# A selective scan on one core: state sums in 64x64 tiles, skip term on TensorE, gating from PSUM on VectorE

## The reference, cut to what matters

```python
xz = einsum('bld,ed->ble', x, inW); xi, z = split(xz, 2)
u = silu(causal_conv4(xi) + convB)
dt, Bm, Cm = split(u @ xpW.T, [8, 24])
delta = softplus(dt @ dtW.T + dtB);  A = -exp(Alog)
h[t] = h[t-1] * exp(delta[t] * A) + delta[t] * u[t] * B[t]      # per channel and state
y[t] = sum over the 16 states of h[t] * C[t]
y = (y + u * Dp) * silu(z);  out = y @ outW.T
```

## Time and profile before

| | us |
|---|---|
| median of three runs (3236.65 to 3239.31) | 3238.32 |
| the profiled execution | 3238.96 |
| its span, first to last instruction | 3237.2 |
| busy in the span: PE, PEld, DVE, ACT, POOL | 2481.1, 1545.4, 2175.4, 1557.8, 1433.7 |
| TensorE clock granted, mean over the span | 0.887 |
| first scan of the Mamba stage starts, last one starts | 1646.3, 2692.5 |

### The profile page before, as it was taken

How to read it: one execution, slowest core, us unless ns; L and a number is a source line. 1 busy time by engine, 2 the same in 40 slices (tenths; PEclk the granted TensorE clock), 3 DMA queues, 4 the chain that set the end, 5 groups by cost and what they waited for, 6 DMA issues and landing times. The chain is left out here.

```text
span 3237.2 us, 54004 instructions
## 1 busy us (share of the span) xinstructions
PE 2481.1 (77%) x18923; PEld 1545.4 (48%) x18923; DVE 2175.4 (67%) x3838; ACT 1557.8 (48%) x2529; POOL 1433.7 (44%) x1159
## 2 busy tenths in 40 slices
PE   4888657764777589899689999999999996553603
PEld 3555435553555455555345555555555553332303
DVE  4787547885777545555356767767677774887688
ACT  4888425553777522222265556555555542221360
POOL 5555235554222100000058877778777874332001
PEclk9999777885999889999899999999999998765756
DMA  1000010000000100000122222122221211000000
GB/s 38 1 0 1 8 34 17 15 10 4 1 0 0 45 1 0 0 0 0 31 66 70 69 67 63 60 74 65 67 63 62 71 61 35 20 13 8 0 0 26
DMA packets 108701, 94.26 MB, mean 29 GB/s; under 512 B 11136, under 2 KB 104976, under 8 KB 108432
## 3 DMA queue, kind: packets, MB, share of 16 engines
q1 hardware_dynamic: 108560, 92.26, 9.4%
HBM read 83.32 MB, written 2.62 MB: 27 GB/s over the span
## 5 line engine op out<-in xcount | busy, mean ns | idle before, releaser
L1919 POOL TENSOR_TENSOR mam_h<-mam_h,mam_c_all 128x1024 f32<-128x1024 f32 x256 | 632.4, 2478 | 187.4 <-DVE mam_h L1987 187.4
L1987 DVE TENSOR_TENSOR_SCAN mam_h<-mam_decay,mam_ps_b 128x1024 f32<-128x1024 f32 x256 | 578.2, 2279 | 199.7 <-PE mam_ps_b L1633 195.5
L1640 PE MATMUL mam_ps_y<-mam_h,all_ident 128*128 128x512 f32 x1024 | 501.4, 613 | 6.1 <-DVE mam_y L1963 6.1
L1803 ACT ACTIVATE mam_decay<-mam_delta,mam_a_neg 128x508 f32<-128x508 f32 x512 | 331.3, 709 | 65.6 <-DVE mam_h L1987 65.5
L1633 PEld LDWEIGHTS mam_ps_b<-mam_diag,mam_duT 64*128 64x128 f32 x4096 | 250.1, 188 | 214.2 <-issue 151.6
L1633 PE MATMUL mam_ps_b<-mam_diag,mam_duT 64*128 64x128 f32 x4096 | 299.0, 286 | 20.5 <-DVE mam_h L1987 16.6
L1640 PEld LDWEIGHTS mam_ps_y<-mam_h,all_ident 128*128 128x128 f32 x1024 | 179.0, 190 | 200.5 <-issue 164.4
L519 DVE TENSOR_REDUCE at_top<-at_ps_s 128x4 f32<-128x512 f32 x256 | 175.0, 683 | 120.1 <-PE at_ps_s L359 120.1
L1234 ACT ACTIVATE moe_silu<-moe_ps_g 128x512 f32<-128x512 f32 x144 | 86.0, 597 | 291.9 <-PE moe_ps_g L1181 263.3
L437 ACT COPY at_probT<-at_ps_t 128x512 f32<-128x512 f32 x256 | 145.1, 588 | 119.0 <-PE at_ps_t L344 118.6
L1184 PE MATMUL moe_ps_u<-moe_ynT,moe_w_up 128*128 128x512 f32 x288 | 159.6, 637 | 36.7 <-DVE moe_hidden L1317 36.7
(11 more groups left out here) (346 smaller groups left out, 4925.3 us busy)
## 6 DMA issues: line engine op xcount, KB each, us to landing
mam_c_all<-mam_c_rows SPq DMA_DIRECT2D x256, 256.0 KB, 3.4
all_x_all<-in_x SPq DMA_DIRECT2D x8, 256.0 KB, 4.8
ret_xg<-all_x_all SPq DMA_DIRECT2D x32, 64.0 KB, 1.8
ret_ctx<-in_ctx SPq DMA_DIRECT2D x32, 64.0 KB, 1.9
mam_xg<-all_x_all SPq DMA_DIRECT2D x8, 256.0 KB, 4.0
xat_xg<-all_x_all SPq DMA_DIRECT2D x8, 256.0 KB, 2.4
xat_ctx<-in_ctx SPq DMA_DIRECT2D x8, 256.0 KB, 2.9
out<-qua_res SPq DMA_DIRECT2D x8, 256.0 KB, 2.3
```

The costliest lines, as they stand in the source:

```text
L1640: last = nc.tensor.matmul(ps_y[:, s % DT, :], c.ident[:], h[:, s % SLOTS, :, n, :, :].rearrange("p o g t -> p g o t"), start=(s < DT and n ...
L1803: last = nc.scalar.activation(decay[:, s % SLOTS, :, n, :, 1:T], src, ACT.Exp, scale=a_neg[:, d, s % DT, st:st + 1])
L1919: nc.gpsimd.tensor_tensor(flat(h[:, slot, :, :, :, :]), flat(h[:, slot, :, :, :, :]), flat(c_all[:, chunk, :, :, :, :]), ALU.mult).then_in ...
L1987: nc.vector.tensor_tensor_scan(row(h[:, s % SLOTS, :, :, :, :]), row(decay[:, s % SLOTS, :, :, :, :]), row(ps_b[:, s % 2, :, :, :, :]), 0. ...
```

## The change

The sums over the states for both channel blocks are made together, once in two steps, from four 64x64 tiles of the array: tile (r, t) takes rows r*64 to r*64+63 of block t's `h` and writes partitions t*64 on of bank r of `ps_y`. So `ps_y` holds the channels in another order (partition t*64+j, bank r), and the gate's columns of inW and the rows of outW are loaded in that order by more, smaller DMAs. The skip term u*Dp becomes four matmuls with diagonal weights `skip_diag`, which start each direction's accumulation. GpSimd's two gating instructions and VectorE's two skip instructions are replaced by one VectorE multiplication of 1024 columns that reads `ps_y`. `h` has 8 slots. Several places of the preparing work move by one to three steps, and `conv` and `output` are issued in halves at two steps.

```diff
+    H_SLOTS = 8
-        y = m.sb("y", [128, DT, GT])
+        skip_diag = m.sb("skip_diag", [128, 2, DT, HT])
...
-            LOADS += [(w_in[:, d, :], q("inW")), ...
-                      (w_out[:, d, :, :], q("outW").rearrange("(t q) n -> q t n", q=128)),
+            LOADS += [(w_in[:, d, 0:DT * 128], q("inW")[:, 0:DT * 128]), ...
+            for r in range(2):
+                at = (DT + r) * 128
+                LOADS.append((w_in[:, d, at:at + 128].rearrange("p (t j) -> p t j", t=DT),
+                              q("inW")[:, DT * 128:].rearrange("p (t r j) -> p t r j", t=DT, r=2)[:, :, r, :]))
+            for t in range(DT):
+                LOADS.append((w_out[t * HT:(t + 1) * HT, d, :, :], q("outW").rearrange("(t r j) n -> t j r n", t=DT, r=2)[t]))
...
-        AT_X, AT_SILU, AT_BC, AT_DELTA, AT_LOG, AT_CONV, AT_Z = 1, 3, 5, (6, 7), (8, 9, 10), (9, 10), (11, 12)
-        AT_DUT = (12, 13)
-        AT_GATE, AT_OUT, AT_TOTAL, AT_ROOT, AT_FINISH = 1, 3, 6, 7, 8
-        LAG = 2
+        AT_X, AT_SILU, AT_BC, AT_DELTA, AT_LOG, AT_CONV, AT_Z = 1, 3, 5, (6, 7), (9, 10, 11), (10, 12), (14, 15)
+        AT_DUT = (13, 14)
+        AT_GATE, AT_OUT, AT_TOTAL, AT_ROOT, AT_FINISH = 2, 4, 6, 7, 8
+        LAG = 3
...
+            def conv(f, d, t, part):
+                bank = (f.bank + f.n) % 2
+                if part == 0:
+                    pe.wait_ge(taken, f.base + f.n + 1)
+                for k in range(part * W // 2, (part + 1) * W // 2):
+                    last = nc.tensor.matmul(ps_t[:, bank, :], w_tap[:, d, k, t * 128:(t + 1) * 128], xT[:, d, :, k:k + T], start=(k == 0), stop=(k == W - 1))
+                if part == 1:
+                    f.next()
+                    last.then_inc(filled, 1)
...
-            def sum_states(q, d, s):
-                pe.wait_ge(hc_ready, q + 1)
+            def skip_states(d):
+                for r in range(2):
+                    rows = slice(r * HT, (r + 1) * HT)
+                    for t in range(DT):
+                        nc.tensor.matmul(ps_y[t * HT:(t + 1) * HT, r, :], skip_diag[rows, d, t, :], u[rows, d, t, :], start=True, stop=False, skip_group_check=True)
+
+            def sum_states(q, s):
+                pe.wait_ge(hc_ready, q + DT)
+                pe.sem_inc(hc_passed, 1)
                 for n in range(C2):
-                    last = nc.tensor.matmul(ps_y[:, s % DT, :], c.ident[:], h[:, s % SLOTS, :, n, :, :].rearrange("p o g t -> p g o t"), start=(s < DT and n == 0),
-                                            stop=(s >= S - DT and n == C2 - 1))
+                    for r in range(2):
+                        rows = slice(r * HT, (r + 1) * HT)
+                        for t in range(DT):
+                            last = nc.tensor.matmul(ps_y[t * HT:(t + 1) * HT, r, :], c.ident[rows, rows],
+                                                    h[rows, (s + t) % H_SLOTS, :, n, :, :].rearrange("p o g t -> p g o t"),
+                                                    start=False, stop=(s >= S - DT and n == C2 - 1), skip_group_check=True)
                 last.then_inc(y_done, 1)
...
-                        if not (first and d == 0 and s < LAG):
+                        if s % DT == 1 and not (first and d == 0 and s < LAG):
                             if s == LAG:
                                 if not (first and d == 0):
-                                    pe.wait_ge(y_read, (i * 2 + d) * DT)
-                            sum_states(q - LAG, d, (s - LAG) % S)
+                                    pe.wait_ge(g_ready, i * 2 + d)
+                                    pe.sem_inc(hc_passed, 1)
+                                skip_states(d)
+                            sum_states(q - LAG, (s - LAG) % S)
...
-                        if s == AT_GATE + 1 and not (first and d == 0):
-                            gating(1 - d, i * 2 + d - 1)
...
-            def skipped(d, n):
-                dve.wait_ge(y_done, (n + 1) * S)
-                for t in range(DT):
-                    nc.vector.scalar_tensor_tensor(out=y[:, t, :], in0=u[:, d, t, :], scalar=d_skip[:, d, t:t + 1], in1=ps_y[:, t, :],
-                                                   op0=ALU.mult, op1=ALU.add).then_inc(y_read, 1)
+            def gating(d, n):
+                dve.wait_ge(y_done, (n + 1) * CH)
+                src = lambda t: t.rearrange("p r (g t) -> p (r g) t", g=G)
+                dst = g[:, d, :, :, :].rearrange("p r g t -> p (r g) t") if d == 0 else bn(g[:, d, 0, 0, T - 1:T], (T, 2 * G), (-1, T))
+                nc.vector.tensor_tensor(dst, src(ps_y[:]), src(sz[:, d, :, :]), ALU.mult).then_inc(g_ready, 1)
...
-                        if not (first and d == 0 and s < SLOTS):
-                            dve.wait_ge(y_done, q - SLOTS + 1)
+                        if not (first and d == 0 and s < H_SLOTS):
+                            dve.wait_ge(y_done, i * S + (d * S + s - H_SLOTS) // DT + 1)
```

More of the change, by code:

```diff
@@ L1453, in mamba @@
         y_done = m.sem("y_done")
-        y_read = m.sem("y_read")
+        halves_made = m.sem("halves_made")
+        hc_passed = m.sem("hc_passed")
         g_ready = m.sem("g_ready")
@@ L1635, in b_rows @@
                 last.then_inc(b_ready, 1)
-            def sum_states(q, d, s):
-                pe.wait_ge(hc_ready, q + 1)
-                for n in range(C2):
-                    last = nc.tensor.matmul(ps_y[:, s % DT, :], c.ident[:], h[:, s % SLOTS, :, n, :, :].rearrange("p o g t -> p g o t"), start=(s < DT and n == 0),
-                                            stop=(s >= S - DT and n == C2 - 1))
-                last.then_inc(y_done, 1)
[L1644 to L1648, removed]
-                        for o in range(2 * DT):
-                            d, t = o // DT, o % DT
-                            last = nc.tensor.matmul(dst[:, b * D:(b + 1) * D], g[:, d, t, b, :], w_out[:, d, t, :],
-                                                    start=(b == 0 and o == 0), stop=(b == G - 1 and o == 2 * DT - 1), skip_group_check=True)
-                    return last
-                fill(f, emit)
+            def skip_states(d):
[3 more added lines that the diff above has]
+                        nc.tensor.matmul(ps_y[t * HT:(t + 1) * HT, r, :], skip_diag[rows, d, t, :], u[rows, d, t, :], start=True, stop=False, skip_group_check=True)
@@ new lines, in output @@
+            def output(f, n, part):
+                bank = (f.bank + f.n) % 2
+                if part == 0:
+                    pe.wait_ge(g_ready, n * 2 + 2)
+                    pe.wait_ge(taken, f.base + f.n + 1)
+                for b in range(part * G // 2, (part + 1) * G // 2):
+                    for o in range(2 * DT):
+                        d, t = o // DT, o % DT
+                        last = nc.tensor.matmul(ps_t[:, bank, b * D:(b + 1) * D], g[:, d, t, b, :], w_out[:, d, t, :],
+                                                start=(b == 0 and o == 0), stop=(b == G - 1 and o == 2 * DT - 1), skip_group_check=True)
+                if part == 1:
+                    f.next()
+                    last.then_inc(filled, 1)
@@ L1712, in _ @@
             for t in range(DT):
-                conv(f, 0, t)
+                conv(f, 0, t, 0)
+                conv(f, 0, t, 1)
             for t in range(DT):
@@ L1722, in _ @@
             for t in range(DT):
-                conv(f, 1, t)
+                conv(f, 1, t, 0)
+                conv(f, 1, t, 1)
             for t in range(DT):
@@ L1735, in _ @@
             f = group(NG - 1, False)
-            output(f, NG - 1)
+            output(f, NG - 1, 0)
+            output(f, NG - 1, 1)
         @block.scalar
@@ L1931, in _ @@
             group(NG - 1, False)
-            gating(1, NG * 2 - 1)
             after.root(nc, pool, c, NG - 1)
@@ L1939, in _ @@
                 nc.vector.tensor_tensor(w_tap[:, d, :, :], w_tap[:, d, :, :], repeat(w_in[:, d, 0:DT * 128], W), ALU.mult).then_inc(prepared, 1)
-            nc.vector.tensor_tensor(halves[:], c.ident[:, 0:HT], c.ident[:, HT:T], ALU.add).then_inc(prepared, 1)
+            nc.vector.tensor_tensor(halves[:], c.ident[:, 0:HT], c.ident[:, HT:T], ALU.add).then_inc(halves_made, 1)
+            dve.wait_ge(halves_made, 1)
+            dve.sem_inc(prepared, 1)
+            for d in range(2):
+                for t in range(DT):
+                    nc.vector.tensor_scalar(skip_diag[:, d, t, :], halves[:], d_skip[:, d, t:t + 1], None, ALU.mult).then_inc(prepared, 1)
             for k in range(len(LOG1P_PAIRS)):
@@ L2016, in _ @@
             group(NG - 1, False, steps)
-            skipped(1, NG * 2 - 1)
+            gating(1, NG * 2 - 1)
             total_of(steps, NG - 1, taken_by(NG - 1, fillings_before(1, S, False) + 1))
```

40 lines of the change are left out of this document (17 added, 23 removed).

## The result

The changed kernel takes 3155.94 us, the median of 4 runs (3142.05 to 3162.35), beside 3238.82 us for the kernel before; the ratio is 0.9733 with a 95% interval of 0.9695 to 0.9771. It is 83 us faster, where 128 were forecast. Its profiled execution took 3142.05 us, the shortest of the four, with a span of 3140.3.

A forecast was written before the change was run, and what follows sets the result against it. TensorE was taken to bound ordinary directions of the Mamba stage, with a second chain of equal length around steps 8 to 12. Directions save 145 us, less 15 for clock, plus 1 elsewhere: 3239 - 130 + 1 = 3110 us, range 3030 to 3175.

The forecast's parts named there:

- The sums and the skip term: TensorE in each direction: 1.91 us a pair of steps, saving 15.3 us a direction; the skip term adds 0.85.
- The two-tile rival: TensorE's sums: only two tiles run at a time, a pair costs 3.62 us, total about 3230 us; chance 7%.
- the draining one: TensorE's sums: the array empties at each change between row halves, a pair costs 4.4 us, total 3340; chance 3%.
- the estimate of 2.2 + 0.2 a pair: TensorE's sums by a skill page's 3.07 times for four row tiles: a direction 4 us more on PE.
- The short direction: Mamba stage, every second direction, without `output` and the norm: 55.9 us forecast for 64 before.
- scan 10 does not wait for ACT's decay: Sign denied here: in each direction scan 10 would wait for ACT's decay, done at 35.35 us of the direction.
- The long direction: Mamba stage, every second direction, with `output` and the norm: 59.0 us forecast for 70 before.
- the clock's 15 us: Mamba stage: 1 us a direction allowed for stretches at half clock in PE's new gaps, 145 becoming 130.
- DVE's norm of the group before fits into that: VectorE in long directions: the norm fits into the 3.1 us by which PE falls back, adding nothing to 58.95.
- The walk: Likeliest case: one direction stepped through the in-order queues, 55.9 and 59.0 us for 64 and 70; chance 60%.
- The clock rival: Mamba stage: TensorE's clock falls twice a direction, 2.6 us more in each of 15, total 3150 us; chance 16%.
- better than the walk: Mamba stage: queues overlap more, a direction is PE's 50 and 54.4 us, total 3035 us; chance 14%.

The follow-up runs named there:

- slots4: The changed kernel with four slots of `h` instead of eight: 3235.44 us, ratio 0.9968 to the kernel before.
- again: The changed kernel measured once more with no edit, as the base for the other runs: 3150.19 us, ratio 0.9712 to the kernel before.
- before_slots8: The kernel before with eight slots of `h`, the rest of its work unchanged: 3240.51 us, ratio 0.9997 to the kernel before.
- no_apply: The changed kernel without the norm's last part (four VectorE instructions), so its output is not the reference's: 3136.46 us.
- both: The changed kernel with TensorE's loop over inner groups written out and the norm's last part moved to ScalarE at step 11: 3118.32 us.
- pe_unrolled: The changed kernel with only TensorE's loop over the six inner groups written out: 3126.83 us, ratio 0.9646 to the kernel before.
- both_whole_conv: The kernel of both, with `conv` issued whole again at steps 10 and 12 instead of in halves: 3105.78 us.
- old_places: The changed kernel with `conv`, `gate`, `turn_du` and the polynomial at their steps of the kernel before: 3135.15 us.
- in_turn: The changed kernel with the two matmuls of one tile issued behind each other, tile after tile: 3161.77 us in one run.

## Why the prediction was right or wrong

**The sums and the skip term: right.** 1.95 us a pair for 1.91, 253.5 us in all where 245 was named; skip 1.09 with a shape change, for 0.85. The two-tile rival (3.62 a pair) and the draining one (4.4) fall with it, and the estimate of 2.2 + 0.2 a pair was too high as well.

**The slots: right in kind, and larger than the text made them.** The sentence "if eight slots of `h` were not there, scans would wait for sums that come up to four steps later" had no price. slots4 gives it one: 3235 for 3150 us, so 85 of the 94 us by which again beats the kernel before. Nor do the slots bring it by themselves (before_slots8). The 8 x 1.91 us a direction that the sums spare TensorE reach the end only because the scans can run ahead of them.

**The short direction: right.** 55.9 forecast, 56.2 measured, and 55.8 in the later versions. In direction 13 PE is busy for 50.0 of 56.1 us (49.9 forecast) and POOL for 51.4 (54.3 forecast). Over the stage POOL is busy for 819 us and stood 115.8 before its products, for 790 and under 100. One thing in it was not so: scan 10 does not wait for ACT's decay. It starts behind DVE's own polynomial, whose part 1 took 3.20 for 1.23 (DVE, then ACT, of direction 13):

```profile
2467.00 1.20 DVE L1974 SCALAR_TENSOR_TENSOR mam_poly<-all_y_all,mam_soft 128x1024 f32<-128x1024 f32 x1
2468.32 3.20 DVE L1974 SCALAR_TENSOR_TENSOR mam_poly<-all_y_all,mam_poly 128x1024 f32<-128x1024 f32 x1
2471.74 2.29 DVE L2011 TENSOR_TENSOR_SCAN mam_h<-mam_decay,mam_ps_b 128x1024 f32<-128x1024 f32 x1 [0.22 <-DVE mam_poly L1974]
...
2469.70 3.75 ACT L1833 ACTIVATE mam_decay<-mam_delta,mam_a_neg 128x508 f32<-128x508 f32 x6
```

The interval came out nearly the same (6.9 for 6.4), and that is luck: the first of ACT's three decays in that row is done by about 2471 (2469.70 + 3.75 / 3), half a microsecond before the polynomial. The text had one of two chains of nearly equal length and called the other free.

**The long direction: wrong, and by two steps.** 59.0 forecast, 66.6 measured. Over the stage, long and short pairs 2 to 13 took 734 us for 689 (45 more), direction 14 took 62.8 for 58 and the last 41 for 45; the first pair and the clock's 15 us taken off, 30 us of the forecast 130 are missing in the profiled execution.
- "DVE's norm of the group before fits into that" and "the moved tables cost nothing by themselves" are one error. The norm's last part fitted the wait at step 8 because the old table had put both there. The walk moved the wait to behind scan 9 and left the norm at 8, where I did not place it: 1.21 waiting for the root and 3.90 for 1.11. Leaving it out takes the interval from 7.62 to 4.08 and gives 3.1 us in direction 2, where nothing else differs (63.1 to 60.0); with the loop written out moving it gives 2.7 a long direction (62.8 to 60.1). In the time it is 14 us (no_apply) or 8 (both).
- The edge of TensorE's loop had no term at all. In the trace of before the branch's record is as long (3.37 to 3.86 us), but the idle time of TensorE behind it is 0.72 to 1.20, and the scan there waits 1.50 to 1.99: `b_rows` and a sum that were already in TensorE's queue ran under most of the jump. In the kernel after it costs 2.6 to 4.2 us in each of the five long directions behind a jump (65.5 to 67.0, for 62.8), 23 us in the time (pe_unrolled).
With both out the walk holds: 60.1 + 55.8 us a pair for 59.0 + 55.9. For a direction of 66.6 that is 3.8 for the edge, 2.7 for the norm and 1.1 unexplained.

**The clock: a small part, with no fixed price.** The mean of the stage's granted clock is 0.97 for 1.00. Between full and half that is 0.03 x 2 x 949, some 57 us at 1.2 GHz, where the kernel before had next to none. In the two short stretches above, 0.57 and 0.72, two `b_rows` took 2.91 for 2.06 and one 2.08 for 1.16, behind an idle of 2.32 and of 3.98 us of PE, as in the earlier trace rows. A short direction with such a stretch in it lasts 1.6 us longer (57.8 for 56.2): one of those from 3 to 13 in the first trace, two in again's, so less than the allowance of 1 us in each. In both_whole_conv long directions with a clock of 0.97 and of 1.00 alike last 60.1; in old_places they last 60.8 at 1.00 and 64.8 at 0.92. The clock rival named 3150 (3155, had it added 0.9 and 1.1 to 2.0 instead of 1.8), near the 3156 measured, and that nearness is luck: it had 2.6 us in every direction, where five of the short ones stand at the forecast and the long ones lose 3.8 to the edge and 2.7 to the norm (66.6, 62.8, 60.1). Of the edge's 3.8 a part can still be the clock's, which falls to half right behind it in directions 6 to 12 (the first short stretch above): direction 4 has the jump and full clock behind it, and lasts 65.5, 2.6 more than without the jump. The rival "better than the walk" has nothing for it: the best version stands at 3106.

**The rest of the sum** is small. From the end of the last scan to the end of the program nothing changed (542.4 us in both), so the 2 us that gating from PSUM was to spare there did not come. The first scan starts 2.3 us later, for 3 and a little forecast, which says nothing, as it varies by more from one trace to the next. Some terms are off by 1 us or less in the adding (6 pairs at 134 less 114.9 are 115, not 116; 71 less 58 is 13). 14 of the 46 us between 3110 and 3156 are the distance of the median from the profiled execution.

**What stays open.** How much of the gain of both_whole_conv is clock and how much shorter `conv`; how much of the edge's cost is the clock behind it; which of the moved entries makes old_places faster, beside the norm; and what makes the records start in fours in in_turn.

## What to carry to other kernels

When the bounding engine is relieved, list what its backlog had covered, loop edges and an in-order helper's small last part among them, and walk the direction that holds these, not the plain one. When a table of steps moves, place every entry that stays, too: one that sat in a wait now sits in front of one. And price a buffer's depth together with the work that it decouples: here the slots alone gave nothing, the changed kernel without them 10 us, and the two together 83 to 94.

## What the runs showed of the hardware

- A taken jump at the end of TensorE's loop is dear: in the kernel after its own record lasts 3.34 to 4.20 us on TensorE (up to 4.82 in again) and 0.04 to 0.07 on the other engines, and `b_rows` behind it starts after 1.81 to 2.67 us of idle "issue". The same branch not taken, at the loop's end, lasts 0.08. The page "Runtime: NRT & Kernel Launch" of the Trainium skill (Instruction fetch mechanics) says that a taken branch out of the fetched stretch must first bring its target's instructions by DMA. That would fit; pe_unrolled shows the cost gone, not its cause.
- Four instructions of 128 columns on VectorE (L155, tensor and scalars from SBUF) take 1.11 us with no GpSimd instruction beside them, and 3.90 beside GpSimd's `diag` and product: 1.07 and 2.40 for the two beside it, 0.34 for each of the two after it. No run here has the same four at step 8 with GpSimd idle, so the contention is read from these rows, not shown by an edit.
- A group of 16 float32 records of 512 columns on four 64x64 tiles takes 1.95 us, the same as 4 records on the full array, and takes 1.97 with the tiles' matmuls in another order.
